# All decay rows of a tile loaded at the end of the tile ahead, and other places for growth rows and o in the last tile of pass 1

## The reference

```python
h = layernorm(x) * (1 + ca) + sa
q, k, v = (h @ Wq.T), (h @ Wk.T), (h @ Wv.T)          # 16 heads of 64
log_decay = -softplus(h @ Wd.T + bd)
k = k * sigmoid(h @ Wg.T)
# per head: s_t = exp(log_decay_t) * s_{t-1} + k_t^T v_t ;  out_t = q_t s_t
out = rms_normalised(out) * norm_w * sigmoid(h @ Wog.T)
x = x + ga * (out @ Wo.T)
h = layernorm(x) * (1 + cb) + sb                      # then a gated, token-shifted FFN
x = x + gb * ffn(h)
```

## Time and profile before

| | us |
|---|---|
| median of 3 runs | 3235.6 (3235.37 to 3236.47) |
| the profiled execution | 3233.8 |
| its span, first to last instruction | 3231.8 |
| PE busy | 3163.1 (98%) |
| DVE busy | 1880.5 (58%) |
| ACT busy | 1294.4 (40%) |
| POOL busy | 474.8 (15%) |
| mean granted clock of TensorE | 0.992 |

### The profile page before, as it was taken

One profiled execution on the slowest core, in us unless ns is written; L12 is line 12 of the kernel. 1 busy time (PEld: TensorE's weight loads), 2 busy tenths in 40 slices (PEclk: granted clock), 3 DMA queues, 4 the chain that ended last, 5 costly groups with the idle time before them and its releaser, 6 DMA issues. The chain is left out here.

```text
span 3231.8 us, 96720 instructions
## 1 busy us (share of the span) xinstructions
PE 3163.1 (98%) x37253; PEld 2966.7 (92%) x37253; DVE 1880.5 (58%) x4823; ACT 1294.4 (40%) x3584; POOL 474.8 (15%) x723
## 2 busy tenths in 40 slices
PE   7999999999999999999999979999999999999999
PEld 6999999999999999999999968999999999999998
DVE  5454554545545555455455456666666666776676
ACT  3444444444444444444444443333333333333332
POOL 0111111111111111111111112111111111111110
PEclk8999999999999999999999989999999999999999
DMA  6132222322223222232222243322222233333220
GB/s 216 58 103 74 89 90 67 105 71 91 90 69 105 68 93 87 71 103 70 94 84 74 88 154 89 81 82 78 78 78 78 79 82 84 83 81 82 81 78 27
DMA packets 273330, 278.93 MB, mean 86 GB/s; under 512 B 24720, under 2 KB 221344, under 8 KB 273072
## 3 DMA queue, kind: packets, MB, share of 16 engines
q1 hardware_dynamic: 270960, 270.67, 27.4%
q10 hardware_dynamic: 2112, 4.19, 0.4%
HBM read 189.84 MB, written 84.93 MB: 85 GB/s over the span
## 5 line engine op out<-in xcount | busy, mean ns | idle before, releaser
L55 PE MATMUL psJ<-h_hi,w_k_hi 128*128 128x256 f32 x1024 | 298.9, 292 | 0.0
L55 PE MATMUL psJ<-h_hi,w_g_hi 128*128 128x256 f32 x1024 | 293.8, 287 | 4.6 <-DVE h_lo L883 2.1
L55 PE MATMUL psJ<-h_hi,w_q_hi 128*128 128x256 f32 x1024 | 296.5, 290 | 0.9 <-issue 0.5
L55 PE MATMUL psG<-h_hi,w_og_hi 128*128 128x256 f32 x1024 | 286.4, 280 | 4.1 <-PEq L348 4.1
L56 PE MATMUL psJ<-h_lo,w_q_hi 128*128 128x256 f32 x1024 | 286.6, 280 | 0.2 <-issue 0.2
L57 PE MATMUL psJ<-h_hi,w_q_lo 128*128 128x256 f32 x1024 | 286.2, 279 | 0.5 <-issue 0.5
L57 PE MATMUL psJ<-h_hi,w_g_lo 128*128 128x256 f32 x1024 | 286.5, 280 | 0.0
L56 PE MATMUL psJ<-h_lo,w_g_hi 128*128 128x256 f32 x1024 | 286.4, 280 | 0.0
L57 PE MATMUL psJ<-h_hi,w_k_lo 128*128 128x256 f32 x1024 | 285.3, 279 | 0.0
L56 PE MATMUL psJ<-h_lo,w_k_hi 128*128 128x256 f32 x1024 | 285.2, 279 | 0.0
L56 PE MATMUL psG<-h_lo,w_og_hi 128*128 128x256 f32 x1024 | 283.6, 277 | 0.0
(11 more groups left out here) (264 smaller groups left out, 9306.0 us busy)
## 6 DMA issues: line engine op xcount, KB each, us to landing
grown<-cum_dram SPq DMA_DIRECT2D x256, 128.0 KB
cum_rows<-cum_dram SPq DMA_DIRECT2D x512, 64.0 KB, 3.5
o_dram<-o SPq DMA_DIRECT2D x256, 128.0 KB, 4.0
o_cols<-o_dram SPq DMA_DIRECT2D x128, 256.0 KB, 4.9
an_norm_x<-in_L_attn_x_dram SPq DMA_DIRECT2D x32, 512.0 KB, 4.2
h_dram<-h_hi SPq DMA_DIRECT2D x32, 512.0 KB, 3.1
h_dram<-h_lo SPq DMA_DIRECT2D x32, 512.0 KB, 3.9
h_hi<-h_dram SPq DMA_DIRECT2D x32, 512.0 KB, 4.0
```

The source lines that it names most:

```text
L55: nc.tensor.matmul(out, w_hi, x_hi, start=first, stop=False)
```

## The change

1. **Decay rows.** All eight pairs are issued at the end of the tile ahead, behind growth rows 0 and 1. `cum_rows` has room for eight pairs, since only half of it was in use; each pair has a semaphore of its own.
2. **The last call.** Growth rows of pairs 2 to 7 are loaded early into places that are no longer used: `gate`, `grown` and `q` of pairs 0 and 1. The output o goes to `kg`, at its own pairs, so ACT's copy of o waits for no store.
3. **Weights in the last call.** TensorE, ACT and DVE turn, round and finish weight 0 in quarter 0, 1 and 2 in quarter 1, 3 and 4 in quarter 2, 5 and 6 in quarter 3. Before it was none, 0 and 1, 2 and 3, 4 and 5, and weight 6 at the end. SP issues the load of weight 1 behind growth rows 4 to 7.

```diff
-        spread = [ctx.enter_context(nc.semaphore(f"a_spread{n}")) for n in range(4)]
+        spread = [ctx.enter_context(nc.semaphore(f"a_spread{n}")) for n in range(NP)]
         grow = [ctx.enter_context(nc.semaphore(f"a_grow{n}")) for n in range(2)]
+        grow_end = [ctx.enter_context(nc.semaphore(f"a_grow_end{n}")) for n in range(1, ND)]
+        grown_end = [grown, gate, grown, q[:, 0:2, :]]
...
         def rows_of(p):
 
-            return cum_rows[:, p % 4, 0:2, :]
+            return cum_rows[:, p % 4, p // 4 * 2:p // 4 * 2 + 2, :]
 
         def spread_rows(sp, i, p):
 
-            hold(sp, s["e"], NP * i + p - 3)
+            hold(sp, s["e"], NP * (i - 1) + p + 1)
...
+        def grow_rows_end(sp, i, d):
+
+            for e in range(2):
+                p = 2 * d + e
+                sp.dma_start(grown_end[d][:, e, :], cum_b[i, 1, 2 * p:2 * p + 2, :].unsqueeze(1).to_broadcast([2, DH, T])
+                             ).then_inc(grow_end[d - 1], 16)
+
+        def o_of(j, d):
+
+            if isinstance(j, int) and j == NT - 1:
+                return kg[:, 2 * d:2 * d + 2, :].rearrange("p e (h t) -> p e h t", h=NC)
+            return o
...
                 if not proj and d == 0:
+                    sp.wait_ge(s["k"], NP * NT)
+                    grow_rows_end(sp, j, 1)
                     sp.wait_ge(s["proj"], NU * NT)
                     sp.wait_ge(s["h_kept"], 32 * NT)
                     load_w(sp, 0)
+                    sp.wait_ge(s["qg"], NP * j + 2)
+                    grow_rows_end(sp, j, 2)
+                    sp.wait_ge(s["score"], ND * j + 1)
+                    grow_rows_end(sp, j, 3)
                     load_w(sp, 1)
...
-                if gla and d < 3:
+                if gla and proj and d < 3:
                     for p in (2 * d, 2 * d + 1):
                         grow_rows(sp, j, p + 2)
-                if gla and d < 2:
-                    for p in (2 * d, 2 * d + 1):
-                        spread_rows(sp, j, p + 4)
...
                 for pair in range(2):
                     grow_rows(sp, i, pair)
-                    spread_rows(sp, i, pair)
-                for pair in range(2, 4):
+                for pair in range(NP):
                     spread_rows(sp, i, pair)
...
-                if not proj and d == 1:
+                if not proj and d == 0:
                     pe.wait_ge(s["by_act"], NA * NT)
-                if not proj and d > 0:
-                    turn_w(pe, 2 * d - 2)
-                    turn_w(pe, 2 * d - 1)
+                if not proj:
+                    for n in range(max(0, 2 * d - 1), 2 * d + 1):
+                        turn_w(pe, n)
...
             for e in range(2):
-                hold(act, store[e], 16 * m)
-                nc.scalar.copy(o[:, e, :, :], psH[e]).then_inc(s["o_part"], 1)
+                if o_of(j, d) is o:
+                    hold(act, store[e], 16 * m)
+                nc.scalar.copy(o_of(j, d)[:, e, :, :], psH[e]).then_inc(s["o_part"], 1)
```

More of the change, by code:

```diff
@@ L440, in spread_rows @@
                              cum_b[i, 0, 2 * p:2 * p + 2, b * CH:(b + 1) * CH].unsqueeze(0).to_broadcast([DH, 2, CH])
-                             ).then_inc(spread[p % 4], 16)
+                             ).then_inc(spread[p], 16)
         def grow_rows(sp, i, p):
@@ L458, in store_o @@
             sp.wait_ge(s["o"], NP * j + p + 1)
-            sp.dma_start(o_v[j, :, p, :, :], o[:, p % 2, :, :]).then_inc(store[p % 2], 16)
+            sp.dma_start(o_v[j, :, p, :, :], o_of(j, p // 2)[:, p % 2, :, :]).then_inc(store[p % 2], 16)
         def sp_tile(sp, i, gla, proj, prep, opens=False):
@@ L718, in _ @@
             pe_tile(pe, NT, True, False, 0)
-            turn_w(pe, NW - 1)
             o_ready(pe, ND * NT - 1)
@@ L829, in act_tile @@
                     decays(act, j, 2 * d + 1)
-                if not proj and d > 0:
-                    for n in (2 * d - 2, 2 * d - 1):
+                if not proj:
+                    for n in range(max(0, 2 * d - 1), 2 * d + 1):
                         round_w(act, n)
@@ L857, in _ @@
             act_tile(act, NT, True, False, 0)
-            round_w(act, NW - 1)
             copy_o(act, NT - 1, ND - 1)
@@ L899, in grow_q @@
                 dve.wait_ge(s["by_act"], act_done(j, ("q", p)))
-                dve.wait_ge(grow[e], 16 * (ND * j + d + 1))
+                at_end = isinstance(j, int) and j == NT - 1 and d > 0
+                if at_end:
+                    dve.wait_ge(grow_end[d - 1], 32)
+                else:
+                    dve.wait_ge(grow[e], 16 * (ND * j + d + 1))
+                factor = grown_end[d] if at_end else grown
                 nc.vector.tensor_tensor(qg[:, e, :].rearrange("p (c b t) -> p c b t", b=2, c=NC),
-                                        q[:, p, :].rearrange("p (c b t) -> p c b t", b=2, c=NC), grown[:, e, :].rearrange(
-                    "p (b c t) -> p c b t", b=2, c=NC), ALU.mult).then_inc(s["qg"], 1)
+                                        q[:, p, :].rearrange("p (c b t) -> p c b t", b=2, c=NC),
+                                        factor[:, e, :].rearrange("p (b c t) -> p c b t", b=2, c=NC),
+                                        ALU.mult).then_inc(s["qg"], 1)
         def weigh_k(dve, j, d):
@@ L950, in sum_o @@
             for e in range(2):
-                nc.vector.tensor_tensor(o[:, e, :, :].rearrange("p h (b t) -> p h b t", b=2),
-                                        o[:, e, :, :].rearrange("p h (b t) -> p h b t", b=2),
-                                        psO[e].rearrange("p b (h t) -> p h b t", h=2), ALU.add).then_inc(s["o"], 1)
+                both = o_of(j, d)[:, e, :, :].rearrange("p h (b t) -> p h b t", b=2)
+                nc.vector.tensor_tensor(both, both, psO[e].rearrange("p b (h t) -> p h b t", h=2),
+                                        ALU.add).then_inc(s["o"], 1)
         def grow_state(dve, j, d):
@@ L1061, in dve_tile @@
                     weigh_k(dve, j, d + 1)
-                if not proj and d > 0:
-                    rest_w(dve, 2 * d - 2)
-                    rest_w(dve, 2 * d - 1)
+                if not proj:
+                    for n in range(max(0, 2 * d - 1), 2 * d + 1):
+                        rest_w(dve, n)
             if proj:
@@ L1086, in _ @@
             dve_tile(dve, NT, False, 0)
-            rest_w(dve, NW - 1)
             sum_o(dve, NT - 1, ND - 1)
@@ L1095, in mask_rows @@
         def mask_rows(pool, i, p):
-            pool.wait_ge(spread[p % 4], 32 * (NP // 4 * i + p // 4 + 1))
+            pool.wait_ge(spread[p], 32 * (i + 1))
             hold(pool, s["mask"], NP * i + p)
```

## The result

The changed kernel takes **3465.0 us** (median of 4 runs, 3462.0 to 3467.7) against 3235.5 before: ratio 1.071, 95% interval 1.0697 to 1.0723. It is 229.5 us slower; the forecast was 3425. The profiled execution has a span of 3465.8 us, 234.0 more than before.

What follows compares the result with a forecast made beforehand. TensorE, busy all of the time in pass 1's loop tiles, was taken as the bound. 28 tiles at 6.3 us (176), plus 12 and 2, gave 190 us: 3425 against 3235.6; own range 3390 to 3480, wide range 3290 to 3500.

Steps and rivals of the forecast that it cites:

- The stall in the loop: Each pass 1 loop tile: later o stores hold ACT's copies and TensorE's g3 of the second quarter, 4.0 to 5.7 us.
- The second path: Loop tile: a late growth row delays DVE's gate that frees q3's bank, near 1452.6, beside the g3 stall.
- The clock: Behind each loop stall TensorE's clock falls, so following work takes 1.3 to 2.6 us longer; 1.7 taken.
- The tiles outside the loop: Three tiles of pass 1 outside the loop: stall about 3.5 us, 4 us each with some clock, 12 us.
- The last tile: Last tile of pass 1: new gaps of 22 us replace four of 21.2; +2 us charged, bounds −6 and +10.
- The first gap: Last tile: TensorE waits for the first weight, whose load comes later behind row transfers and growth rows; 14 us.
- The second: Last tile: TensorE waits for the second weight, loaded behind four more growth rows and scaled near 1921.5; 8 us.
- the further gaps: Last tile: the causes of its four old stalls (21.2 us) are removed; the rest shortens as little as it grows.
- eight masks in one piece: Sign expected in the changed profile: GpSimd does all eight masks in one piece; no time was given.
- The faster rival's rule: Growth rows land 2.3 us after issue, o stores about 1443.7, so no loop stall: 3227 us in all; chance 0.08.

Runs made afterwards that it cites:

- e1: The kernel before with the decay rows of the change alone, its last call in the old order: 3461.8 us, ratio 1.0693.
- e2: The changed kernel with the decay rows put back as before, the last call keeping its new order: 3243.9 us, ratio 1.0021.
- e5: The changed kernel with growth rows of two pairs loaded by two DMAs, one per half of the partitions (64 rows outermost instead of 2): 3295.3 us, ratio 1.0183.
- e6: The changed kernel with decay rows in six DMAs (groups of 2, 2 and 4 pairs), the first group between growth rows 0 and 1: 3256.4 us, ratio 1.0066.
- e9: The changed kernel with six DMAs of decay rows, all behind growth rows loaded by halves of the partitions: 3221.9 us, ratio 0.9957.
- e4: The changed kernel with other places for o in even quarters, so ACT's copy no longer waits for the store: 3444.1 us, ratio 1.0638.
- e7: The changed kernel with six decay-row DMAs, growth rows by halves, and loads of weights 0 and 1 ahead of the last call's growth rows: 3220.9 us, ratio 0.9952.
- e3: The changed kernel with a tile's decay rows loaded by 4 DMAs of four pairs each instead of 16 of one pair: 3356.7 us, ratio 1.0365.

## Why the prediction was right, and what it mis-sized

**The stall in the loop.** Right in place, cause and order. The h store came 15.0 us after the first growth row in the tile shown (1392.90 to 1407.89), 15.5 at the median ("about 15"), sixteen issues in 12.85 us ("about 12.5"), the first o store landing 9.9 us after the growth rows' issue (9.7 to 10.8), TensorE idle before g3 of the second quarter, released by ACT's copy of q. e1 and e2 show that it is the decay rows; e5, e6 and e9 that it is the issues and the two engines together. The mean idle before g3 is 5.2 us, within the bounds of 4.0 to 5.7, against 4.6 taken. ACT's copy of o waited for the store 6.7 us on the mean, where "some 5 us" was forecast.

**The second path.** "It lies beside the first stall" is what e4 showed: with the wait for the store gone, DVE's gate holds TensorE for 3.2 us in each tile. That the growth rows also hold ACT's copy of q the prediction did not name.

**The clock.** The granted clock falls behind each stall as forecast. The term was mis-sized: 1.7 us taken; a loop tile is 7.5 us longer with 5.3 more of idle time, so 2.2 us. Both terms of the tile were too small, the idle time by 0.7 us and the clock by 0.5. They give 211.1 us for the 28 tiles, where the sum had 176. This is 35 of the 44 us between the forecast's 190 and the 234.0 of the profile.

**The tiles outside the loop.** 12 us taken, 8.8 measured.

**The last tile.** Here the mechanism was wrong in part: "together 22 us against 21.2, and the rest shortens as little as it grows". The first gap was right (14 forecast, 15.07). The second was put at 8 us and came to 13.31: the second weight landed at 2143.6 and was scaled by 2146.3, and counted from the last projection of v that is 5 us later than the forecast. The four growth rows do hold their engines as the sum said: while SP was issuing them, the 16 DMA engines were 14% busy and moved 48 GB/s, as for a growth row alone.

```profile
2126.00:2130.00 4.00, 3.90 (x28) 3.50 (x32) 1.83 (x3) 1.98 (x4) 0.00 (x0) 0.50 0.14 48
```

Two things are not in the sum. SP could issue the second weight only at 2128.68, since issuing the four growth rows took it 11.4 us; and its 1 MB then took 14.9 us to land, beside ACT's load of another weight and two stores of o:

```profile
2129.79 0.43 ACTq L284 DMA_DIRECT2D w_stage<-in_L_attn_Wo_dram  x1
2143.66 2.69 POOL L292 TENSOR_SCALAR m_rows<-w_stage,c_ga 128x512 f32<-128x512 f32 x4 [28.93 <-DMA w_stage<-in_L_attn_Wo_dram]
```

How much each of the two adds no run separates. And the forecast took the further gaps as removed, but 7.1 us of new ones stand there (0.89, 3.26 and 2.96), which TensorE spends waiting for DVE to finish a weight. In e7, where the loads of weights 0 and 1 come first, the last two are still 3.60 and 2.96 us, so they seem to belong to the new order of the weights' work and not to late loads; no run changes that order alone. The call is 13.9 us longer in place of 2, beyond the upper bound of 10.

The errors hardly cancel: the loop is 35 us and the last tile 12 us above the forecast, the tiles outside the loop 3 us below it, and 3465 lies within the forecast's own range of 3390 to 3480.

**GpSimd** did not do its eight masks in one piece: six, then, after a step of the norm, pairs 6 and 7 from 1437.96 on. Nothing waited for these.

**The faster rival's rule**, a landing 2.3 us after the issue of a growth row by the Trainium skill's "SBUF — State Buffer", section "The DMA setup-cost knee (why "@ 1 MiB" ≠ asymptote)", did not hold for these rows: the second growth row was used 9.7 us after the pair's first issue, as the earlier trace rows had told. Its figure is near only once the shape is changed (2.9 to 3.0 us in e5).

## What to carry to other kernels

Count each DMA twice: once as time of the queue that issues it, here 0.65 to 0.8 us for a load of decay rows, of 64 or of 256 KB (the plain 512 KB stores of h took 0.33 to 0.36), and once as time of the DMA engines it runs on. A small broadcast with outermost dimension 2 held two of sixteen engines, and the store behind it took 7.8 us to land in place of 3.9. When a group of transfers is to come earlier, merge it first (but leave the first-needed piece small) and look at what was behind it on the queue. A stall with two causes does not respond to a test of one as a sum would: try both alone and together.

## What was not expected of the hardware

- **An issue can take five times as long when earlier DMAs are pending.** The same growth-row DMA took SP 0.53 us each for the first two of the last call and 2.6 and 3.1 us on the mean for the next four (minimum, median and maximum in ns below), near the 2.8 us that it holds its engines:

```profile
L456 SPq DMA_DIRECT2D gate<-cum_dram x2: 529/532/534, 2115.0 to 2115.5; - x2
L456 SPq DMA_DIRECT2D grown<-cum_dram x2: 1678/2616/3555, 2117.2 to 2118.9; - x2
L456 SPq DMA_DIRECT2D q<-cum_dram x2: 2561/3054/3548, 2122.5 to 2126.1; - x2
```

  With 64 outermost, in e5, the same six issues took 0.59 to 0.61 us each. That a queue was full behind the two engines is argued from these durations; no run tested it by itself.

- **The same gap costs the clock or does not.** In e3 TensorE idled 2.08 us before 658.30 and 2.09 us before 1025.37, at the same place of two tiles. The 4 us behind (granted clock third from the end):

```profile
658.20:662.20 4.00, 3.90 (x20) 3.90 (x21) 0.67 (x2) 1.40 (x6) 3.24 (x7) 0.57 0.32 110
1025.30:1029.30 4.00, 3.93 (x35) 3.94 (x35) 0.63 (x2) 2.25 (x9) 3.21 (x7) 1.00 0.32 109
```

  The first stretch ran mostly at 1.2 GHz (granted clock 0.57), with 20 matmuls where the other did 35 at 2.4 GHz; these tiles took 60.9 and 59.3 us, from one g3 to the next. So the same stall has a price of 1.6 us in one tile and none in another, and a mean over tiles is needed to read it. What decides it no run here shows.

- **A DMA of 256 KB is issued as fast as one of 64 KB.** In e7's last tile six DMAs of 128 and 256 KB took SP 3.91 us, 0.65 each; in the changed kernel's last tile sixteen of 64 KB took 10.99, 0.69 each. First e7, then the changed kernel:

```profile
1881.56 3.91 SPq L441 DMA_DIRECT2D cum_rows<-cum_dram  x6
2103.91 10.99 SPq L441 DMA_DIRECT2D cum_rows<-cum_dram  x16
```
